# An attention block with routed experts on one core: step tables redrawn, a nine-slot ring for the final gathers, one dense batch moved ahead of the next projection

## What is computed

```python
x = _layernorm(x + _L0_attn_ref(x, ...))          # 16 x 512 x 256
shared = _silu(X @ sW1 + sb1) @ sW2 + sb2
logits = einsum('btd,ed->bte', X, routing_W) + expert_bias
top_vals, top_idx = top_k(sqrt(softplus(logits)), 2)
hdn = _silu(einsum('nd,edh->enh', Xf, rW1) + rb1[:, None, :])
y = einsum('enh,ehd->end', hdn, rW2) + rb2[:, None, :]
routed = einsum('ne,end->nd', combine, y)
x = _layernorm(x + shared + routed)
```

## Time and profile before

| what | value |
|---|---|
| median of three runs | 1660.95 us |
| lowest, highest | 1656.72, 1667.56 us |
| the profiled execution | 1663.59 us |
| its span in the trace | 1661.8 us |
| mean granted TensorE clock | 0.936 of 2.4 GHz |
| busy: PE, DVE, ACT, POOL | 88%, 71%, 61%, 44% |
| instructions | 33130 |

### The profile page before, as it was taken

The page is one execution under the profiler, slowest core; times in us unless marked ns, Lnnn a source line. Parts: engine busy times, 40 slices in busy tenths (PEclk is TensorE's granted clock), DMA queues, the critical chain, the costliest instruction groups (busy, mean ns, idle before and its releaser), DMA issues.

```text
span 1661.8 us, 33130 instructions
## 1 busy us (share of the span) xinstructions
PE 1458.4 (88%) x11110; PEld 801.2 (48%) x11110; DVE 1171.7 (71%) x2631; ACT 1019.3 (61%) x1742; POOL 723.9 (44%) x655
## 2 busy tenths in 40 slices
PE   7987999999999889899999899988888999896467
PEld 4433444444444435555555544454455555564345
DVE  7665777878778787666666677857776577645674
ACT  1465666666767656666677576666566587675242
POOL 2233353635545343541535253533666344255630
PEclk8789899999999989999999999999999899998789
DMA  7334243434343324454545433443566566686531
GB/s 208 115 109 147 91 124 101 129 108 132 102 123 116 115 92 141 132 175 139 178 138 165 130 120 116 128 139 120 166 214 222 177 217 209 192 257 212 168 106 51
DMA packets 185349, 242.00 MB, mean 146 GB/s; under 512 B 67239, under 2 KB 104190, under 8 KB 185182
## 3 DMA queue, kind: packets, MB, share of 16 engines
q1 hardware_dynamic: 154746, 181.18, 36.4%
q0 software_dynamic: 10752, 29.37, 5.4%
q10 hardware_dynamic: 19684, 29.33, 5.0%
HBM read 152.53 MB, written 91.44 MB: 147 GB/s over the span
## 4 chain that ended last, share of the span: by engine, by line
PE 51%; DVE 15%; SPq 14%; DMA 10%; issue 6%; POOL 2%; ACT 2%; POOLq 0%; ACTq 0%; DVEq 0%
PE pS L641 15%; PE pV L683 9%; PE pG L707 6%; DVE negm L932 5%; PE pG L729 3%; PE pG L716 3%; SPq L390 2%; DMA xg<-d_x 2%; PE pS L647 2%; DMA d_rec<-scr 2%; PE pG L810 2%; SPq L459 2%; PE pG L818 2%; SPq L499 1%; DMA d_sum<-pvs 1%
## 5 line engine op out<-in xcount | busy, mean ns | idle before, releaser
L932 DVE TENSOR_REDUCE negm<-pS 128x1 f32<-128x512 f32 x1024 | 659.6, 683 | 336.4 <-PE pS L647 329.6
L1368 ACT ACTIVATE ee<-pT,slp 128x512 f32<-128x512 f32 x1024 | 649.0, 684 | 216.8 <-PE pT L668 215.2
L641 PE MATMUL pS<-ka,qa 62*128 62x512 f32 x1024 | 485.4, 509 | 81.0 <-DVE negm L932 68.3
L662 PE MATMUL pT<-qa,ka 64*128 64x512 f32 x1024 | 480.9, 504 | 0.2 <-ACT ee L1368 0.2
L641 PEld LDWEIGHTS pS<-ka,qa 62*128 62x128 f32 x1024 | 198.4, 194 | 330.0 <-issue 312.8
L683 PE MATMUL pV<-ee,vv 128*32 128x512 f32 (+1 forms) x2048 | 286.8, 633 | 0.0
L647 PE MATMUL pS<-mAB,tri 64*128 64x64 bf16 x2048 | 243.6, 200 | 0.0
L668 PE MATMUL pT<-mAB,tri 64*128 64x64 bf16 x2048 | 239.9, 198 | 0.0
L1555 POOL TENSOR_TENSOR raw<-raw,rope 128x512 f32<-128x512 f32 x61 | 78.2, 1282 | 330.0 <-DVE sh L966 329.9
L662 PEld LDWEIGHTS pT<-qa,ka 64*128 64x128 f32 x1024 | 195.6, 191 | 4.5 <-issue 3.1
L647 PEld LDWEIGHTS pS<-mAB,tri 64*128 64x128 bf16 x2048 | 119.8, 99 | 139.6 <-issue 107.3
(11 more groups left out here) (186 smaller groups left out, 2192.8 us busy)
## 6 DMA issues: line engine op xcount, KB each, us to landing
d_part<-parts SPq DMA_DIRECT2D x63, 512.0 KB, 2.8
qa<-d_part SPq DMA_DIRECT2D x378, 64.0 KB
wb<-in_wb SPq DMA_DIRECT2D x77, 256.5 KB
xg<-d_x SPq DMA_DIRECT2D x77, 256.0 KB, 2.9
d_y<-yb ACTq DMA_DIRECT2D x77, 256.0 KB, 2.6
ka<-d_part SPq DMA_DIRECT2D x128, 128.0 KB
xT<-in_xT SPq DMA_DIRECT2D x16, 512.0 KB
ka<-d_part SPq DMA_DIRECT2D x128, 64.0 KB
```

Source lines behind the costliest of these rows:

```text
L641: e.matmul(pS[:, k, :], qa[g % 4][r, i, t * 128:t * 128 + 128].bitcast(F32R), ka[g % 4][r, i, :].bitcast(F32R), start=True, stop=False)
L662: e.matmul(pT[:, k, :], ka[g % 4][r, i, kt * 128:kt * 128 + 128].bitcast(F32R), qa[g % 4][r, i, :].bitcast(F32R), start=True, stop=False)
L932: e.tensor_reduce(negm[:, g % 2, j, t + k:t + k + 1], pS[:, k, :], AX, ALU.max, negate=True).then_inc(s_max, 1)
L1368: e.activation(ee[:, k, d % 7, :], pT[:, k, :], ACT.Exp, scale=slp[:, 6, h:h + 1]).then_inc(s_exp, 1)
```

## The change

The table gets other numbers, so that jobs of a batch stand at other steps. The finals of groups 1 and 2 (batches 6 to 13) gather into a ring of nine buffers: the three of before and six that lie in tiles of the attention which is over by then (`raw`, `sh`, and halves of `qa0` and `ka0`); those of batches 0 to 5 keep the three. Their steps get an own row in `FINAL_STEPS`: all four gathers in the first two steps, the adds three steps later than before. Batch 14's experts move to steps 530 to 537 and batch 15's to 560 to 567, so the first now stand ahead of batch 15's projection (541, 542, 545). More idle matmuls stand at the start.

```diff
 QK = ((-23, -22), (-18, -17), (-11, -7), (-5, -1))
-SHUFFLE = (2, 2, 2, 2)
-ROPE = (1, 1, 1, 3, 3)
-PARTS_OUT = 5
-V = ((10, 12), (15, 17))
+SHUFFLE = (2, 2, 2, 6)
+ROPE = (1, 1, 1, 2, 2)
+PARTS_OUT = 4
+V = ((2, 3), (5, 11))
...
-ASSEMBLE = -6
-M_SPLIT, M_OUT, M_IN = (-1, -1, 2)
+ASSEMBLE = -4
+M_SPLIT, M_OUT, M_IN = (-1, 0, 3)
...
-BIASX = 55
-PROJ = ((58, 61), (65, 65))
+BIASX = 59
+PROJ = ((61, 61), (62, 65))
...
-GATE = 83
-DOWN = (87, 89)
-BASE_OUT = 93
+GATE = 85
+DOWN = (87, 87)
+BASE_OUT = 100
...
-FINALS_AT = ((278, 13), (158, 5), (125, 6))
+FINALS_AT = ((278,13,6,356,13),(158,5,6,300,5),(126,5,2,156,6))
...
-DENSE_AT = ((93, 1), (86, 1))
-LOADD, GATED, DOWND = (-5, 1, 2)
-WEIGHTS, VAR3, NORM3, OUTD = (0, 24, 25, 27)
-BASE_IN, GATHER, ADD, VAR2, NORM2, OUT = (-1, (1, 2, 2, 4), (3, 4, 5, 6), 6, 8, 9)
-LATE, PREP, PADS = 11, (18, 20, 22, 24), 40
-
-WARM = (5, 6, 4, 4, 5)
+DENSE_AT = ((82,1),(80,1))
+LOADD, GATED, DOWND = (-16, 1, 2)
+WEIGHTS, VAR3, NORM3, OUTD = (-1, 21, 23, 24)
+
+BASE_IN, GATHER, ADD, VAR2, NORM2, OUT = range(6)
+FINAL_STEPS = ((-1, (1, 2, 2, 4), (3, 4, 5, 6), 6, 8, 9), (2, (0, 0, 1, 1), (6, 7, 8, 9), 9, 10, 11))
+LATE, PREP, PADS = (6, (18, 20, 20, 22), 38)
+
+WARM = (6, 9, 6, 6, 7)
...
+def gathered(k):
+
+    if k < FIRST_LATE:
+        return k % NGG, k // NGG + 1
+    i, n = (k - FIRST_LATE) % NGL, (k - FIRST_LATE) // NGL + 1
+    return i, n + (len(range(i, FIRST_LATE, NGG)) if i < NGG else 0)
...
+    ggl = [x[:, :, :] for x in gg] + [x[:, :].rearrange("p (k c) -> p k c", k=2) for x in (raw, sh)]
+    ggl += [x[0][:, i, :].rearrange("p (k c) -> p k c", k=2) for x in (qa, ka) for i in range(2)]
...
-            if k > 2:
+            i, held = gathered(k)
+            if k >= FIRST_LATE + NGL:
+                e.wait_ge(s_add, k - NGL + 1)
+            elif k >= FIRST_LATE:
+                if k < FIRST_LATE + NGG:
+                    e.wait_ge(s_add, FIRST_LATE)
+                elif k < FIRST_LATE + NGG + 2:
+                    e.wait_ge(s_part, 4 * NB)
+                else:
+                    e.wait_ge(s_t, 16 * (4 * NB - 3))
+            elif k > 2:
                 e.wait_ge(s_add, k - 2)
```

More of the change, by code:

```diff
@@ L53 @@
 TOP2 = (74, 75)
-RANK = 77
+RANK = 76
 PLACE = 77
-SCATTER = (78, 79, 80, 81, 82, 83, 84, 85)
-UP = (77, 78)
-GATE = 83
-DOWN = (87, 89)
-BASE_OUT = 93
+SCATTER = (78, 79, 80, 81, 82, 83, 84, 84)
+UP = (76, 77)
+GATE = 85
+DOWN = (87, 87)
+BASE_OUT = 100
 EXPS = 76
@@ L100 @@
             for g, (at, per, n, at2, per2) in enumerate(BLOCKS_AT) for j in range(NBLOCKS[g])}
-FINAL_OF = {32 * LAST_OF[g] + at + int(k * per): LAST_OF[g] + 1 - GROUPS[g] + k
-            for g, (at, per) in enumerate(FINALS_AT) for k in range(GROUPS[g])}
+FINAL_OF = {32 * LAST_OF[g] + (at + int(k * per) if k < n else at2 + int((k - n) * per2)): LAST_OF[g] + 1 - GROUPS[g] + k
+            for g, (at, per, n, at2, per2) in enumerate(FINALS_AT) for k in range(GROUPS[g])}
+NGG, NGL = 3, 9
+FIRST_LATE = 4 * GROUPS[0]
 DENSE_OF = {32 * (SPARSE + k) + at + x * per: E * k + x for k, (at, per) in enumerate(DENSE_AT) for x in range(E)}
@@ L143, in block_due, with final_due @@
     return BLOCK_OF.get(s - at, -1)
-def final_due(s, at):
-    return FINAL_OF.get(s - at, -1)
+def final_due(s, step, t=0):
+    for kind, steps in enumerate(FINAL_STEPS):
+        at = steps[step][t] if step in (GATHER, ADD) else steps[step]
+        b = FINAL_OF.get(s - at, -1)
+        if b >= 0 and (b >= GROUPS[0]) == (kind == 1):
+            return b
+    return -1
+def gathered(k):
[3 more added lines that the diff above has]
+    return i, n + (len(range(i, FIRST_LATE, NGG)) if i < NGG else 0)
 def dense_due(s, at):
@@ L280, in _build @@
     comb = sb("comb", [128, 2, DENSE, 4, E])
-    gg = [sb(f"gg{i}", [128, 2, C]) for i in range(3)]
+    gg = [sb(f"gg{i}", [128, 2, C]) for i in range(NGG)]
     bs = [sb(f"bs{i}", [128, 4, C]) for i in range(2)]
@@ L329, in _build @@
     bs_in = [sem(f"bs_in{i}") for i in range(2)]
-    gg_in = [sem(f"gg_in{i}") for i in range(3)]
+    gg_in = [sem(f"gg_in{i}") for i in range(NGL)]
     xg_in = [sem(f"xg_in{i}") for i in range(NX)]
@@ L1190, in add_experts @@
                 e.wait_ge(bs_in[b % 2], 16 * (b // 2 + 1))
[L1191 to L1192 removed]
+            i, n = gathered(k)
+            e.wait_ge(gg_in[i], 32 * n)
+            link(e.scalar_tensor_tensor(x_, ggl[i][:, 0, :], wts[:, b, 0, t:t + 1], x_, ALU.mult, ALU.add))
             linked()
[L1194 removed]
+            e.scalar_tensor_tensor(x_, ggl[i][:, 1, :], wts[:, b, 1, t:t + 1], x_, ALU.mult, ALU.add).then_inc(s_add, 1)
             e.wait_ge(s_add, k + 1)
```

19 lines of the change are left out of this document (8 added, 11 removed).

## The result

Twelve runs of each kernel, side by side: the kernel before took 1659.51 us (1656.72 to 1667.56), the changed one 1670.97 us (1664.04 to 1680.03). The ratio is 1.008, with a 95% interval of 1.006 to 1.0099. That is some 11 us more, where 29 less were predicted; the profiled executions differ by 6.4 us (spans of 1661.8 and 1668.2).

A forecast was written before the change was run, and what follows sets the result against it. PE was taken to bound ordinary batches, with waits for block rows in block batches and cross-engine waits in the tail. 1663.6 - 20 - 10 - 3 + 0.8 = 1631.4 us; range 1608 to 1656.

The forecast's parts named there:

- up to the first maximum: At the start, four more warm matmuls ahead of the first scores: +0.8 us, ends +2 and -9.
- The ordinary batches: V at earlier positions fills PE's waits for row maxima: net 1.3 us in about eight batches, booked -10, ends +8 and -25.
- Assembly on SP: In SP's queue, block loads go out ahead of the ten assembly transfers, so PE waits less for rows: -3 us.
- Rival (c): Assembly transfers on SP come late, each of 60 head groups waits about 1 us: about 1692 us; chance 0.08.
- The tail: After the last exponentials, the new order of finals and dense experts saves 20 us; ends 0 and -32.
- the start of batch 14's experts: In the tail, the first expert's first add starts at about 1528 us, bounds 1519 and 1545.
- their eight periods: Batch 14's eight experts need near 30 us, PE 3.91 us each, so the last down matmuls end at about 1558.
- All behind the projection: After batch 15's projection: 15.3 us to its first normalization, 20.9 to the power, then the experts; end at 1641.1.
- the collision: POOL's bias addition slowed DVE's `pvs` scaling; now it would hit the finals' adds at 2.2 us once: no term.
- (b): The tail gains little, as DVE interleaves finals with sixteen experts: tail 6, batches 8, giving 1650 us; chance 0.17.
- (a): The table is neutral, waits move to positions 12 to 17, and only the tail gains 20: 1643 us; chance 0.16.
- (d): PE's clock drops after positions 2 and 3 vanish and the start stays higher: 8 + 8 more, 1615 us; chance 0.13.

The follow-up runs named there:

- g2_ring_only: The kernel before with the ring of nine alone and every step as before; 1661.15 us, ratio 1.0016 to the kernel before.
- g3_early_gather: The kernel before with the ring of nine and all gathers in a final's first two steps, base load and adds unmoved; 1651.19 us, ratio 0.9942.
- e3_v: The kernel before with only v, the shuffle, the rotation and the parts' write at their new places; 1663.93 us, ratio 1.0019.
- e1_asm: The changed kernel with the assembly and the maxima at their old places; 1656.84 us, ratio 0.9955 to the kernel before.
- f4_asm: The same kernel as e1_asm, run again beside the changed kernel (1726.88 us there); 1703.05 us, ratio 1.0145 to the kernel before.
- series A: First and fourth groups of experiments, where the kernel before took 1662.1 and 1658.7 us and the changed kernel stands at 1.009.
- g1_after_rec: The changed kernel with REC_IN back at 6 alone; 1665.95 us, ratio 1.0041 to the kernel before.
- g4_after: The changed kernel itself, run and traced a second time as a yardstick; 1674.68 us, ratio 1.009 to the kernel before.
- series B: Second, third and fifth groups of experiments, where the kernel before took 1680.1, 1677.3 and 1678.5 us and the changed kernel stands at 1.027.
- f2_ring: The kernel before with only the ring of nine and the finals' new steps, dense order as before; 1698.29 us, ratio 1.0118.
- f1_dense: The kernel before with only the steps of the two dense batches changed, finals and ring of three as before; 1689.54 us, ratio 1.0066.
- k1_repaired: The changed kernel with assembly, maxima, REC_IN and the finals' base load and adds put back, ring and early gathers kept; 1686.62 us, ratio 1.0045.
- e5_rec: The changed kernel with assembly and maxima at their old places and REC_IN 6; 1691.15 us, ratio 1.0056 to the kernel before.
- e8_tail: The kernel before with only the changed tail: dense batches' steps, finals' steps and ring of nine; 1687.94 us, ratio 1.0039.

## Why the prediction was wrong, step by step

The forecast of 1631.4 us, term by term, against the two traces, each stretch from first maximum to first maximum:

| stretch | forecast | measured |
|---|---|---|
| up to the first maximum | +0.8 | +1.9 |
| batches 0 to 7, 11, 12 | -10 | -21.7 |
| batches 8 to 10 and 13 | -3 | +18.3 |
| batch 14 | 0 | +0.2 |
| batch 15 to its last exponentials | 0 | +16.9 |
| from there to the end | -20 | -9.3 |

The miss of 38.6 us (1670.0 instead of 1631.4) is thus 21 in the batches with blocks, 17 in batch 15 ahead of its last exponentials and 11 in the tail, less the 12 that the other batches gained beyond the forecast.

**The ordinary batches, -10.** Right in sign, and its size isn't known well: the stretches without blocks took 783.5 us before, but 775.7 and 776.2 in g2_ring_only and g3_early_gather, which run the same order up to step 509, and 761.8 and 763.3 in the two traces of the changed kernel. The gain is so between 12 and 22 us. The wait for maxima fell from 17.3 to 9.7 us in batches 3 to 6, and the new wait at position 17 came, at 0.5 to 1.7 us instead of 0.5. That v is the reason isn't shown: e3_v has 775.5 us.

**Assembly on SP, -3.** This is the step that failed in sign, and the costliest. The argument "a block's load now goes out ahead of these ten instead of behind" was right, and the waits for rows fell by 9.1 us in batches 8 to 10. What it left out is who stands behind: the ten transfers now come after the load, and PE waited 16.1 us for them there where it had not waited at all. It also took the new order of the queue for free ("the wait for the sums is merely put ahead of the maxima"): from the sums' write to their read SP spent 1.5 us before and 2.7 now, on average over 64 groups. The 4.4 us of slack were read in batch 4, which has no block loads, and used for all stages. Rival (c) named this very wait and priced it for every group; it came in the batches with blocks, not in the ordinary ones, where 0.7 us were lost. (Its 3.4 us for two steps don't fit its own rows: two of 32 steps of a batch of 75 us are 4.7, more than the slack.) In batch 13 the loss shows as waits for the maxima instead, 14.4 us in 4 places where it was 8.5 in 5; since e1_asm takes it back too (103.6 us), it comes from the same two lines, but the way isn't traced. It was given 0.08 because "the issue follows from waits, not from steps". Yet moving a step changes what stands ahead of a write and so how long SP waits for it: SP's three waits grew from 236.4 to 311.7 us, and are 267.2 in e1_asm. By e1_asm and f4_asm this part is worth 18 to 24 us: without it the forecast's sign would have been right in series A, its size not.

**REC_IN.** The prediction didn't price it at all: one step less, in a queue of which it said "SP isn't paced by steps, only by its waits". It is worth 8.7 us (g1_after_rec against g4_after).

**The tail, -20.** After the last exponentials 9.3 us were gained. Counted from the last exponentials, what was forecast and what came:

| | forecast | measured |
|---|---|---|
| batch 8's rstd on POOL | 8 | 12.6 |
| batch 14's first dense add | 16 | 24.3 |
| pair | 39 | 46.8 |
| projection | 46 | 57.5 |
| projection to batch 15's normalization | 15.3 | 17.4 |
| from there to the power | 20.9 | 19.5 |
| power's start to the end | 46.9 | 46.0 |

So the mis-sized terms are the start of batch 14's experts (8.3 us late) and their eight periods: from the first add to the projection 33.2 us (1552.15 to 1585.35) instead of 30. The first goes back to POOL's waits for DVE's variances: 15 us were allowed for batches 6 and 7, and they came to 26.4 (16.32 ahead of 1500.85 and 10.12 ahead of 1526.66). All behind the projection was right to about 2 us. The picture that the term began with was wrong as well: in the kernel before POOL waited little for adds (5.9 us, above), and the ring of nine alone gained nothing (g2_ring_only). One stall is the collision that the prediction had read and priced at 2.2 us in another place: the gate of 1574.80 took 4.07 us instead of 0.68, beside POOL's pair and bias, and PE waited 3.52 for it. The Trainium skill (GPSIMD Engine Reference, section 8, Key points) warns of contention with DVE instructions that have two SBUF inputs; the rows agree. The prediction called it no term because the bias was thought to meet the finals' adds. It met the instruction for which PE waits.

**What no step covered.** Batch 15 up to its last exponentials, +16.9 us. The sum started at the last exponentials and assumed that they stay where they are. Taking back the assembly (193.0), the dense loads (192.2), or the dense order (194.1) leaves this stretch as it is; single parts on the kernel before give 182.3 (e3_v), 179.5 (g2_ring_only) and 183.0 (g3_early_gather), against 177.1. What it is made of can be read: PE waited 22.5 us for block rows here in 9 places instead of 13.6 in 8 (g4_after: 24.7), which is 8.9 of the 10.0 us of added idle time, and the other 6.9 us are busy time at the lower clock. Which number makes the rows late stays open. In series B f2_ring's 197.1 against f1_dense's 185.6 points at the finals' later steps, but k1_repaired, with the adds back at their old steps, has 206.7 where e5_rec, without that, has 205.9. Why every kernel with the new tail gives back here a part of what it gains behind is as open.

**Rivals.** (b) had the tail's term nearest, 6 us against 9.3 measured; (a) kept the full 20 and fell with it; the higher level of the clock in (d) didn't come (0.99 instead of 0.98 in the ordinary batches, lower in batches 13 and 15). On the kernel before, the whole of the new tail gave 1.0039 (e8_tail). The range ended at 1656 because the slower case was one mechanism with a small chance, and two others on the same queue, the sums' longer round trip and REC_IN, weren't in it.

## What to carry to other kernels

Slack that is read in one stage holds for that stage only: before a job is moved in a queue that all stages share, read its distance to its use in the fullest stage. In a queue that writes to HBM and reads back, look at what is issued directly ahead of the write: here the same 8 KB came back after 1.5 us behind small reads and after 4.0 us behind a write of 512 KB. Judge a change to the end of a program from the start of the last full stage, not from the point at which the chain is first bare, and move a wait only when you know what will be waited for next.
